# A fused graph, attention and expert kernel: five raw weight buffers in a ring and four rounded pairs, with the warming matmuls, one small round of transposes and the last transfers rearranged

## The reference

```python
xn = layernorm(x)
x = x + gnn0(xn) + attention0(xn)
x = x + ffn0(layernorm(x))                    # 8 experts, each takes its 32 most probable tokens
xn = layernorm(x)
x = x + gnn1(xn) + attention1(xn)
xn = layernorm(x)                             # from here: layer 1, feed-forward part
gate = xn @ gate_w + routing_bias
top_v, top_i = top_k(gate, 4)                 # 16 experts, 4 chosen for each token
weights = softmax over the chosen, 0 elsewhere
def swiglu(x, w1, w2, w3):
    a = x @ w1
    return a * sigmoid(a) * (x @ w2) @ w3
out = swiglu(xn, sw1, sw2, sw3)               # shared expert
for e in range(16):
    out = out + swiglu(xn, w1[e], w2[e], w3[e]) * weights[:, e:e + 1]
x = x + out
```

## Time and profile before

| | |
|---|---|
| median of 3 runs | 480.98 us |
| profiled execution, own time | 480.59 us |
| its span | 478.8 us |
| granted TensorE clock, mean | 0.993 |
| TensorE matmul busy | 466.4 us (97%) |
| TensorE weight load busy | 297.7 us (62%) |
| VectorE / ScalarE busy | 259.1 us (54%) / 188.2 us (39%) |
| DMA | 191.77 MB, mean 401 GB/s |

### The profile page before, as it was taken

One profiled execution on the slowest core, in us unless ns is written; L12 is line 12 of the kernel. 1 busy time (PEld: TensorE's weight loads), 2 busy tenths in 40 slices (PEclk: granted clock), 3 DMA queues, 4 the chain that ended last, 5 costly groups with the idle time before them and its releaser, 6 DMA issues.

```text
span 478.8 us, 6562 instructions
## 1 busy us (share of the span) xinstructions
PE 466.4 (97%) x2620; PEld 297.7 (62%) x2620; DVE 259.1 (54%) x339; ACT 188.2 (39%) x215; POOL 7.6 (2%) x39
## 2 busy tenths in 40 slices
PE   7989899999999999999999999999999999999997
PEld 4747433446776676666767666666677766667653
DVE  6644440026698375744666385564557467446413
ACT  1020100014775366345554443564544355465110
POOL 2000000001000000000000000000000000000000
PEclk9998899999999999999999999999999999999999
DMA  8999999999969898999999999999999999999994
GB/s 329 429 428 426 426 430 424 424 415 414 420 233 399 348 424 351 371 389 416 429 408 426 422 390 422 423 425 420 426 420 393 415 420 421 418 419 425 421 414 168
DMA packets 25090, 191.77 MB, mean 401 GB/s; under 512 B 2762, under 2 KB 3146, under 8 KB 12900
## 3 DMA queue, kind: packets, MB, share of 16 engines
q1 hardware_dynamic: 24864, 191.21, 96.9%
q10 hardware_dynamic: 196, 0.14, 0.1%
HBM read 191.08 MB, written 0.26 MB: 400 GB/s over the span
## 4 chain that ended last, share of the span: by engine, by line
PE 94%; DVE 3%; ACT 1%; DMA 1%; issue 1%; POOL 0%; DVEq 0%; POOLq 0%
PE ps L1786 17%; PE ps L1808 16%; PE ps L1874 13%; PE ps L1889 9%; PE ps L1793 8%; PE ps L1436 4%; PE ps L1600 3%; PE ps L1856 2%; PE ps L1631 2%; PE ps L1617 2%; PE ps L1429 1%; PE ps L1498 1%; PE ps L1896 1%; PE ps L1860 1%; PE ps L1488 1%; PE ps L1822 1%
## 5 line engine op out<-in xcount | busy, mean ns | idle before, releaser
L1020 DVE TENSOR_TENSOR s_lo<-w_all,s_hi 128x1365 fp32r<-128x1365 f32 x64 | 98.4, 1576 | 50.6 <-ACT s_hi L758 50.4
L758 ACT CAST s_hi<-w_all 128x1365 fp32r<-128x1365 f32 x64 | 82.6, 1331 | 42.6 <-DMA w_all<-in_w 37.7
L1808 PE MATMUL ps<-w_all,exS 128*64 128x512 f32 (+1 forms) x512 | 78.9, 455 | 0.0
L1786 PE MATMUL ps<-s_hi,xT_hi 128*128 128x512 f32 (+1 forms) x192 | 75.5, 393 | 0.7 <-ACT spread_last L815 0.6
L1786 PE MATMUL ps<-s_lo,xT_hi 128*128 128x512 f32 (+1 forms) x192 | 70.4, 369 | 0.0
L1808 PEld LDWEIGHTS ps<-w_all,exS 128*64 128x64 f32 x512 | 34.6, 137 | 43.4 <-issue 43.2
L771 ACT CAST s_hi<-w_raw 128x1536 fp32r<-128x1536 f32 (+1 forms) x32 | 43.6, 1371 | 40.6 <-DMA w_raw<-in_w 40.6
L1034 DVE TENSOR_TENSOR s_lo<-w_raw,s_hi 128x1536 fp32r<-128x1536 f32 (+1 forms) x32 | 51.0, 1613 | 0.0
L1793 PE MATMUL ps<-s_hi,xT_lo 128*128 128x512 f32 (+1 forms) x192 | 50.3, 370 | 0.0
L1889 PE MATMUL ps<-w_raw,hTS 128*64 128x512 f32 (+1 forms) x176 | 45.6, 602 | 0.0
L1786 PEld LDWEIGHTS ps<-s_hi,xT_hi 128*128 128x128 f32 x192 | 36.0, 188 | 12.5 <-issue 3.4
(11 more groups left out here) (339 smaller groups left out, 486.8 us busy)
## 6 DMA issues: line engine op xcount, KB each, us to landing
w_all<-in_w SPq DMA_DIRECT2D x62, 1368.0 KB, 9.7
w_set<-in_w SPq DMA_DIRECT2D x15, 2048.0 KB, 24.9
w_raw<-in_w SPq DMA_DIRECT2D x24, 768.0 KB, 8.5
w_raw<-in_w3s SPq DMA_DIRECT2D x24, 768.0 KB, 10.9
w_all<-in_sw SPq DMA_DIRECT2D x4, 1368.0 KB, 20.8
w_raw<-in_w SPq DMA_DIRECT2D x8, 512.0 KB, 9.2
w_raw<-in_w3s SPq DMA_DIRECT2D x8, 512.0 KB, 12.1
w_last<-in_w SPq DMA_DIRECT2D x2, 1368.0 KB, 10.9
```

Of the source, the lines that this page charges most:

```text
L758: a.copy(s_hi[pair_of(g)][:, 0:F1], raw[:, 0:F1]).then_inc(hi_ready, 1)
L1020: v.tensor_tensor(s_lo[pair][:, 0:F1], raw[:, 0:F1], s_hi[pair][:, 0:F1].bitcast(F32), ALU.subtract).then_inc(lo_ready, 1)
L1786: mm(bank(i + c0 // D)[:, 0:n], xT_hi[:, k], w[:, c0:c0 + n], start=(k == 0 and w is s_hi[pair_of(g)]), stop=False)
L1808: last = mm(bank(NC * part + c0 // D)[FEW * g:FEW * g + FEW, 0:n], exS[:, k, tokens], w[:, CW * g + c0:CW * g + c0 + n], start=(k == 0), s ...
```

## The change

1. `PAIRS_N` becomes 4: the fifth pair's place (slot 3) becomes a fifth raw buffer of two row blocks. The halves of w1 and w2 of all experts go round through the five (`raw_no`, `raw_of`, `landed`), so a transfer waits for the half five transfers before. The first use of the new place waits for the k and v projections, whose weights lie there.
2. The warming matmuls ahead of the last set's tiles are 6, 0, 4 and 2 instead of 0, 2, 2 and 2 (`WARM`).
3. The third spread (one tile) moves from m = 1 to m = 3, into bank 2; the second goes to bank 5 and waits for `hT_lo_ready`. TensorE's wait for all rounds moves to the end of m = 3, and the first `down_few` waits for `spread_lo_ready` instead.
4. The last expert's w3 comes in three transfers (`LAST_DOWN`) into two pairs that lie side by side, once all units are multiplied; the last h is transposed before the step u = 2 instead of u = 3.

```diff
+LAST_DOWN = [(0, 4), (4, 4), (8, FT - 8)]
-PAIRS_N = 5
+PAIRS_N = 4
+RAW_N = 5
+WARM = [6, 0, 4, 2]
-    pair_at = [c.at, c.at + size_pair, at_tail, at_tail + size_pair, slot_at(3)]
+    pair_at = [c.at, c.at + size_pair, at_tail, at_tail + size_pair]
-    LAST_PAIRS = [1, 2, 3, 4]
+    raw_more = place("raw_more", [P, ROWS, HALVES * CW], F32, slot_at(3))
+    raw_units = [t[:, ROWS * j:ROWS * j + ROWS] for t in (w1_all, w2_all) for j in range(KT // ROWS)] + [raw_more[:]]
+    LAST_PAIRS = [0, 1, 2, 3]
+    w3_last = place("w3_last", [P, FT, D], F32, pair_at[LAST_PAIRS[2]])
-    rounds = [bank(i) for i in (2, 2, 2, 2, 7, 2, 7)]
+    rounds = [bank(i) for i in (2, 2, 2, 2, 7, 5, 2)]
+    def raw_no(e, part, k):
+        return 2 * (KT // ROWS) * e + (KT // ROWS) * part + k // ROWS
+    def raw_of(e, part, k):
+        return raw_units[raw_no(e, part, k) % RAW_N][:, k % ROWS]
+    def landed(e, part, k):
+        n = raw_no(e, part, k)
+        return ld_raw[n % RAW_N], 16 * (n // RAW_N + 1)
...
             def next_up(m, part, w):
                 for j in range(KT // ROWS):
-                    wait_unused(m - 1, part, ROWS * j + ROWS - 1)
-                    load_up((w1_all, w2_all)[part], ld_up[part], w, j)
+                    n = raw_no(m, part, ROWS * j) - RAW_N
+                    if n < 0:
+                        sp.wait_ge(k_ps, 2)
+                        sp.wait_ge(v_ps, 2)
+                    else:
+                        each = KT // ROWS
+                        wait_unused(n // (2 * each), n // each % 2, ROWS * (n % each) + ROWS - 1)
+                    load_up(m, part, j, w)
...
-                for u, (t0, n) in enumerate(DOWN):
-                    sp.wait_ge(used, pair_done(LAST_PAIRS[KT // ROWS + u // 2]))
-                    sp.dma_start(w3_last[u][:], w[:, t0:t0 + n]).then_inc(ld_last_down[u], 16)
+                sp.wait_ge(used, len(unit_of))
+                for u, (t0, n) in enumerate(LAST_DOWN):
+                    sp.dma_start(w3_last[:, t0:t0 + n], w[:, t0:t0 + n]).then_inc(ld_last_down[u], 16)
...
             clear_pads(range(PAIRS_N))
-            pool.wait_ge(q_ps, 2)
-            clear_pads(range(4, PAIRS_N))
...
-            for b in range(len(SPREADS)):
+            for b in range(len(SPREADS) - 1):
                 hi_w1(2, b)
                 copy_spread(b)
...
                     end_full(m - 1)
+                    if m == 3:
+                        copy_spread(len(SPREADS) - 1)
...
             for t in range(KT):
-                if t > 0:
-                    keep_warm_briefly(2, 0)
+                keep_warm_briefly(WARM[t], 0)
                 ffn_down_halves(1, t)
...
                 if u == 0:
-                    pe.wait_ge(y_few_ready, few_no(e)) if few_no(e) > 0 else pe.wait_ge(round_ready, ROUNDS)
+                    pe.wait_ge(y_few_ready, few_no(e)) if few_no(e) > 0 else pe.wait_ge(spread_lo_ready, 2)
...
-                if b == 2:
-                    pe.wait_ge(spread_lo_ready, 1)
+                if b == 1:
+                    pe.wait_ge(hT_lo_ready, NC)
...
                 up_part(m, 0, 1)
+                if m == 3:
+                    spread_few(len(SPREADS) - 1)
...
-                    if m == NE - 1 and u == W3_UNITS - 1:
+                    if m == NE - 1 and u == W3_UNITS // 2:
                         turn_last()
...
-                    elif m == 1:
+                    elif m == 1 and u < len(SPREADS):
                         spread_few(u - 1)
...
-                if m == 1:
+                if m == 3:
                     pe.wait_ge(round_ready, ROUNDS)
-                    pe.wait_ge(spread_lo_ready, 2)
...
-            for u, (t0, n) in enumerate(DOWN):
+            for u, (t0, n) in enumerate(LAST_DOWN):
                 pe.wait_ge(ld_last_down[u], 16)
                 for b in range(2):
                     for i in range(t0, t0 + n):
-                        last = down_least(b, u, i)
-                    if u == W3_UNITS - 1:
+                        last = down_least(b, i)
+                    if u == len(LAST_DOWN) - 1:
                         last.then_inc(last_ps, 1)
                 if u == 1:
                     add_few(last_e - 1)
```

More of the change, by code:

```diff
@@ L161, in gps_kernel @@
     s_lo = [place(f"s_lo{i}", [P, SLOT], F32R, at + SLOT * 4) for i, at in enumerate(pair_at)]
-    LAST_PAIRS = [1, 2, 3, 4]
+    raw_more = place("raw_more", [P, ROWS, HALVES * CW], F32, slot_at(3))
+    raw_units = [t[:, ROWS * j:ROWS * j + ROWS] for t in (w1_all, w2_all) for j in range(KT // ROWS)] + [raw_more[:]]
+    assert len(raw_units) == RAW_N
+    LAST_PAIRS = [0, 1, 2, 3]
+    assert pair_at[3] == pair_at[2] + size_pair and FT * D <= 4 * SLOT
     w2_last = [place(f"w2_last{j}", [P, ROWS, HALVES * CW], F32, pair_at[LAST_PAIRS[j]]) for j in range(KT // ROWS)]
-    w3_last = [place(f"w3_last{u}", [P, n, D], F32, pair_at[LAST_PAIRS[KT // ROWS + u // 2]] + u % 2 * SLOT * 4)
-               for u, (_, n) in enumerate(DOWN)]
-    assert max(n for _, n in DOWN) * D <= SLOT and ROWS * HALVES * CW <= 2 * SLOT
+    w3_last = place("w3_last", [P, FT, D], F32, pair_at[LAST_PAIRS[2]])
+    assert ROWS * HALVES * CW <= 2 * SLOT
     c = Cursor(slot_at(3) + size_pair)
@@ L374, in gps_kernel @@
     ld_first_experts = sem("ld_first_experts")
-    ld_up = [[sem(f"ld_w{w}_{j}") for j in range(KT // ROWS)] for w in (1, 2)]
+    ld_raw = [sem(f"ld_raw{i}") for i in range(RAW_N)]
     ld_down = [sem(f"ld_w3_{u}") for u in range(W3_UNITS)]
@@ L378, in gps_kernel @@
     ld_last_up = [sem(f"ld_w2_last{j}") for j in range(KT // ROWS)]
-    ld_last_down = [sem(f"ld_w3_last{u}") for u in range(W3_UNITS)]
+    ld_last_down = [sem(f"ld_w3_last{u}") for u in range(len(LAST_DOWN))]
     consts = sem("consts")
@@ L534, in _, with load_up @@
                     load_set(g, r, w, j)
[L536 to L540, removed]
+            def load_up(m, part, j, w):
+                n = raw_no(m, part, ROWS * j)
+                sp.dma_start(raw_units[n % RAW_N], w[:, ROWS * j:ROWS * j + ROWS]).then_inc(ld_raw[n % RAW_N], 16)
+            for t, (to, w, arrived) in enumerate(((wk1_sb, wk1, ld_k), (wv1_sb, wv1, ld_v), (wq1_sb, wq1, ld_q))):
                 sp.wait_ge(ffn_used, used_of(set_no(0, 1, 1), t))
-                sp.dma_start(to[:], w).then_inc(landed, 16)
+                sp.dma_start(to[:], w).then_inc(arrived, 16)
             sp.wait_ge(ffn_used, used_of(set_no(1, 1, 0), KT - 1))
-            load_up(w1_all, ld_up[0], sw1, 0)
+            load_up(0, 0, 0, sw1)
             sp.dma_start(gnn_w_sb[:], gnn_w).then_inc(ld_gnn_w, 16)
@@ L657, in _ @@
             pool.wait_ge(ffn0_ps, 2)
-            clear_pads(range(4))
+            clear_pads(range(PAIRS_N))
             pool.wait_ge(ld_small, 16)
@@ L750, in _, with hi_up @@
                 a.copy(x2[:, HALF[b]], x2_ps[b]).then_inc(x2_ready, 1)
-            def hi_up(g, raw, landed, e):
-                act.wait_ge(landed, 16 * (e + 1))
+            def hi_up(g, raw, arrived):
+                act.wait_ge(*arrived)
                 if g >= PAIRS_N:
@@ L884, in _ @@
                 if is_full(m):
-                    for k in range(len(SPREADS) if m == 2 else 0, KT):
+                    for k in range(len(SPREADS) - 1 if m == 2 else 0, KT):
                         hi_w1(m, k)
@@ L1022, in lo_w1 @@
             def lo_w1(e, k):
-                lo_up(unit_w1(e, k), w1_raw[k])
+                lo_up(unit_w1(e, k), raw_of(e, 0, k))
             def lo_w2(e, k):
-                lo_up(unit_w2(e, k), w2_raw[k])
+                lo_up(unit_w2(e, k), raw_of(e, 1, k))
             def lo_w3(e, u):
@@ L1801, in up_few @@
             def up_few(e, part, k):
-                pe.wait_ge(ld_up[part][k // ROWS], 16 * (e + 1))
-                w = (w1_raw, w2_raw)[part][k]
+                pe.wait_ge(*landed(e, part, k))
+                w = raw_of(e, part, k)
                 tokens = slice(FEW * few_no(e), FEW * few_no(e) + FEW)
@@ L1814, in up_least @@
                 if part == 0:
-                    pe.wait_ge(ld_up[part][k // ROWS], 16 * (e + 1))
+                    pe.wait_ge(*landed(e, part, k))
                 else:
                     pe.wait_ge(ld_last_up[k // ROWS], 16)
-                w = w1_raw[k] if part == 0 else w2_last[k // ROWS][:, k % ROWS]
+                w = raw_of(e, part, k) if part == 0 else w2_last[k // ROWS][:, k % ROWS]
                 tokens = slice(FEW * few_no(e), FEW * few_no(e) + LEAST)
```

13 lines of the change are left out of this document (6 added, 7 removed).

## The result

| | before | after |
|---|---|---|
| median, same chip, 22 runs each | 481.69 us | 478.09 us (477.39 to 481.5) |
| ratio, 95% interval | | 0.9947 [0.9936, 0.9958] |
| profiled execution, own time | 480.59 us | 478.98 us |
| its span, mean clock | 478.8 us, 0.993 | 477.2 us, 0.993 |

What follows compares the result with a forecast made beforehand. The prediction took TensorE's order of matmuls to bound the kernel from about 137 us on. Its terms, +1.32 - 0.65 - 0.3 + 0 = +0.37 us on the median of 480.98, gave 481.3 us, with an 8-in-10 range of 479.5 to 482.6.

Steps and rivals of the forecast that it cites:

- What bounds: From about 137 us on, the order of TensorE's matmuls is the limit, not the DMA.
- D: Transfers limit from 137 us on, so earlier ones make it faster: 474.7 us at best, 477 if half returns; chance 0.07.
- Part 1: Warming matmuls between 97 and 103 us, ahead of the last down set's tiles: +1.32 us, at most +1.92.
- there is no waiting left to put warmers into: TensorE reaches the last set's last tile, at 102.13 us, just as its data lands, so added warmers delay it.
- Part 2: Last spread moved from m = 1 to m = 3: hole before m = 2 closed, -0.65 us, bounds -0.84 and 0.
- the return: The moved spread's transpose comes back at m = 3, costing 0.11 to 0.27 us, taken as 0.19.
- the ring: Fifth raw buffer lets transfers be issued one unit earlier: 0 us, bounds -0.3 and 0.
- Part 3: The end: w3 in three transfers, add_few after eight tiles: -0.3 us, bounds -0.35 and 0; moving the transposes 0.
- The wait of add_few: Near 472 us add_few waits 0.25 to 0.3 us behind 24 instructions; 32 ahead would remove it.
- Part 4: Four pairs (bounds 0 and +0.8 us) and five raw buffers (bounds -0.3 and 0): 0 us together.
- rival E: w3's buffers block SP's queue first, so transfer lead stays: same 481.3 us; chance counted within the forecast's 0.58.
- Rival A: Later warmers delay routed transfers, so the end waits 0.6 to 0.9 us for w3's last landing: 482.1 us; chance 0.12.

Runs made afterwards that it cites:

- b_warm: The kernel before with only the new warming matmuls (6, 0, 4, 2): 480.6 us, ratio 0.9994 to before.
- b_spread: The kernel before with only the third spread moved from m = 1 to m = 3: 479.46 us, ratio 0.9978 to before.
- a_old_end: The kernel after with the last h's transposes and the last w3's four transfers as before: 479.99 us, ratio 0.9978 to before.
- a_ring_spread: The kernel after with old warmers, old turn and old w3 pieces, keeping four pairs, five raw buffers and the moved spread: 480.26 us, ratio 0.999 to before.
- b_but_ring: The kernel after with five pairs and the old raw buffers, all else of the change kept: 479.03 us, ratio 0.9956 to before.
- after_again: The kernel after, unchanged, measured in a second series beside its own runs of before: 479.29 us, ratio 0.997 to before.
- b_turn: The kernel before with only the last h transposed before step u = 2 instead of u = 3: 479.67 us, ratio 0.9974 to before.
- a_no_warm: The kernel after with the old warming matmuls (0, 2, 2, 2): 478.54 us, ratio 0.9944 to before.
- a_warm_none: The kernel after with no warming matmuls ahead of the last set's tiles: 477.7 us, ratio 0.9944 to before.
- a_warm_6: The kernel after with only the first group of warming matmuls (6, 0, 0, 0): 477.72 us, ratio 0.9932 to before.
- a_warm_602: The kernel after with warming matmuls (6, 0, 2, 0): 478.46 us, ratio 0.9948 to before.

## Why the prediction was wrong, step by step

- **What bounds.** Right: TensorE's order from 137 us on. A pair of experts still takes all of its 40.70 us in matmuls, and D was wrong: the transfers ran ahead and nothing came of it. The Trainium skill's rule (Perfetto Trace Analysis, Identifying the Most-Contended Engine), that matmul busy time doesn't say how near TensorE is to its roofline, holds all the same: at a share of 97 to 98% and with no idle time the end still got 1.6 us shorter. What the runs don't bear out is to hand the role to the DMA for that.
- **Part 1, +1.32: a step that failed.** The price was right to 0.03 us (3.27 against 3.24). What failed is "there is no waiting left to put warmers into" and "a gain by a higher clock is excluded". Both were read off one execution, in which TensorE happened to come late to the set. In others there is a hole of 1.4 us and a fall of the clock behind it. Measured alone, the term is -0.3 us, with an interval from -1.1 to +0.5 (b_warm, 0.9994): +1.32 is out, the sign is open.
- **Part 2, -0.65.** Right in mechanism, somewhat small. The next up matmul came 0.65 us earlier and not 0.84, but the six behind the hole got 0.28 faster, which had not been counted; the return was taken as 0.19 and is 0.11. Measured -0.9 (b_spread) and -0.75 (with the ring). That the sum of 0.65 came so near is in part luck.
- **Part 3, -0.3: the step that failed in its mechanism.** "The move of the transposes: 0" and three pieces at nothing. Measured -1.6 us in the traces (11.65 to 10.06; 1.5 by span - F of a_old_end against after), 0.85 by the turn and 0.74 by the pieces. The wait of add_few, the only thing priced, was no wait: "about 1.6 us" for the 24 instructions stands in no row, they take 1.85, and behind them, as behind 32 in 1.86, it follows without a hole. That the term had the right sign is luck. Both edits leave every instruction in number and length; they change which of them stand next to one another, and the chain of before had a sign of it: behind the turn two tiles (4 instructions) took 2.06 us, where nine ahead of it took 4.44.
- **Part 4, 0.** Right, to the 0.1 to 0.2 us that the traces can tell: b_spread against a_ring_spread, and b_but_ring against after_again. Its signs came too: the first expert's last four casts of w1 and w2 in ACT's row start at 132.4, 134.2, 138.3 and 140.5 us (133, 135, 139 and 141 forecast), and from 150 to 440 us SP now waits more for w3's buffers (113.5 us in all, 56.4 before) and less for those of w1 and w2 (112.5, 166.7 before), as rival E had it.
- **Rival A** was real in one part, a wait of the end for its landings (b_turn, after_again, b_but_ring), at 0.2 to 0.9 us, and only once the end had become shorter.

The sum by the measured terms: -0.3 - 0.9 + 0.1 - 1.5 = -2.6 us, against the measured -2.5 of the first series and -1.4 of the second. The warmers' term alone is uncertain by 0.8 us either way, so the agreement with the first is no proof; what parts the two series stays open but for the 0.35 us of after_again's wait. By the forecast's terms it was +0.37; of the 3.0 between them, 1.6 are the warmers' cover, 1.2 the end and 0.25 the spread, less 0.1 for the ring.

## What to carry to other kernels

Where matmuls use half or a quarter of the array's columns, their price is per group of neighbours that fill it, not per instruction: before an interposed transpose or a cut between pieces is moved, count which pairs and fours it breaks. What one profile says of slack next to a landing holds for that execution: look at the arrival times of both sides in several before a cover is called gone. And a busy share of 97% with no idle time says that the order of the engine is the bound, not that its work can't get shorter.

## What was not expected of the hardware

- 20 matmul instructions of 128*64 at 600 ns each cost 5.6 us of busy time in one order and 4.7 in another; 44 of 128*32 at 383 ns cost 3.8 us in pieces of three tiles and 3.0 in pieces of four.
- A hole of 1.41 us on TensorE, waiting for a transfer, was followed by a granted clock of 0.52 from 97.5 to 101 us (b_turn; b_spread 0.53 and a_no_warm 0.51 in the same stretch). In a_warm_none the same hole, with two more behind it, was followed by 1.00: the hole alone does not decide it, and what does stays open.
- after, a_warm_6, a_warm_none and a_no_warm are the same program up to the last set, and so is a_warm_602, yet TensorE was free for it between 95.3 and 95.5 us in three of them, at 96.7 in after and at 98.9 in a_warm_602. The clock from 36 to 60 us was 0.93 to 1.00 in the three, 0.89 in after and 0.83 in a_warm_602. What makes the clock fall there was not tried.
